# Bias of the output projection on VectorE, gate behind it on GpSimd, and another rule for the order of TensorE's work

## What is computed

```python
xn = layernorm(x)                                   # x: 4 x 2048 x 256, no affine part
q, k, v = split(xn @ w_qkv + b_qkv)                 # 16 heads of 16
scores = where(j >= i, q @ k.T / 4, -inf)           # each token sees itself and what comes later
s = softmax(scores) @ v  ->  @ w_out + b_out
h = concat([xn, -xn]); h = relu(s0 * (h @ +-k0)) * 2
h = relu(s1 * (h @ +-k1)) * 2
g = silu(s2 * (h @ +-k2))                           # k0, k1, k2: booleans read as +1 and -1
out = x + s * g
```

## Time and profile before

| | |
|---|---|
| median of 3 runs | 2306.75 us (2304.43 to 2308.47) |
| the profiled execution | 2308.26 us, its span 2306.4 us |
| busy: PE, DVE, ACT, POOL | 97%, 78%, 69%, 40% of the span |
| granted TensorE clock | 0.989 of full speed on average |

### The profile page before, as it was taken

The page is one execution under the profiler, slowest core; times in us unless marked ns, Lnnn a source line. Parts: engine busy times, 40 slices in busy tenths (PEclk is TensorE's granted clock), DMA queues, the critical chain, the costliest instruction groups (busy, mean ns, idle before and its releaser), DMA issues.

```text
span 2306.4 us, 60918 instructions
## 1 busy us (share of the span) xinstructions
PE 2228.7 (97%) x23760; PEld 1536.8 (67%) x23760; DVE 1808.4 (78%) x4514; ACT 1580.3 (69%) x3199; POOL 912.1 (40%) x1080
## 2 busy tenths in 40 slices
PE   7998999999999999999999999999999999999886
PEld 6887766666666666676676666666666666666553
DVE  7776788888888888888888888788878787888642
ACT  5663567777777777676777677777777675776573
POOL 1005334333343435343444435343443443354433
PEclk9999999999999999999999999999999999999997
DMA  8985102111111313131221312131312212222222
GB/s 306 357 316 174 43 23 57 32 46 41 52 45 38 95 46 93 37 85 54 79 60 44 88 47 82 44 94 42 86 46 52 86 45 72 59 84 70 75 77 80
DMA packets 157844, 193.31 MB, mean 84 GB/s; under 512 B 65276, under 2 KB 102076, under 8 KB 157560
## 3 DMA queue, kind: packets, MB, share of 16 engines
q1 hardware_dynamic: 156600, 189.41, 27.0%
q10 hardware_dynamic: 960, 0.00, 0.0%
HBM read 112.13 MB, written 76.14 MB: 82 GB/s over the span
## 4 chain that ended last, share of the span: by engine, by line
PE 83%; DMA 5%; DVE 4%; POOL 2%; issue 2%; ACT 2%; SPq 2%; ACTq 0%; POOLq 0%; DVEq 0%
PE b_ps L1437 25%; PE b_pv_ps L1403 22%; PE b_ps L1374 15%; PE b_ps L1384 11%; PE b_ps L1433 5%; DMA a_xs<-L_attn_x 3%; PE b_ps L1458 3%; DVE b_part_max L1549 1%; DVE a_stats L397 1%; ACT b_u L1523 1%; DVE a_qk_parts L435 1%; PE a_qk_ps L291 1%; PE b_ps L1391 1%; POOL b_u_lo L1303 1%; ACT b_probs L1492 1%
## 5 line engine op out<-in xcount | busy, mean ns | idle before, releaser
L1492 ACT ACTIVATE b_probs<-b_ps 128x512 f32<-128x512 f32 (+3 forms) x2560 | 1258.2, 537 | 585.0 <-PE b_ps L1374 554.0
L1549 DVE TENSOR_REDUCE b_part_max<-b_ps 128x1 f32<-128x512 f32 x1536 | 971.6, 680 | 175.0 <-PE b_ps L1384 168.4
L1384 PE MATMUL b_ps<-k_kst,k_qst 48*128 48x512 f32 (+3 forms) x2560 | 894.9, 390 | 10.4 <-DVE b_part_max L1546 4.0
L1374 PE MATMUL b_ps<-k_qst,k_kst 50*128 50x512 f32 (+3 forms) x2560 | 891.4, 389 | 1.1 <-ACT b_probs L1492 0.8
L1374 PEld LDWEIGHTS b_ps<-k_qst,k_kst 50*128 50x128 f32 x2560 | 431.7, 185 | 315.2 <-DVE b_part_max L1549 115.5
L1546 DVE CUSTOM_DVE_ANT_0 b_ps<-b_ps,k_mask 128x512 f32<-128x512 f32 (+3 forms) x1024 | 483.2, 512 | 155.6 <-PE b_ps L1384 149.4
L1403 PE MATMUL b_pv_ps<-b_probs,k_vst 128*32 128x512 f32 (+3 forms) x5120 | 598.9, 542 | 1.9 <-issue 1.7
L1437 PE MATMUL b_ps<-b_u_hi,k_w 64*128 64x256 f32 x4096 | 585.8, 280 | 2.4 <-ACT b_u L1523 0.9
L1437 PE MATMUL b_ps<-b_u_lo,k_w 64*128 64x256 f32 x4096 | 584.0, 279 | 0.0
L1384 PEld LDWEIGHTS b_ps<-k_kst,k_qst 48*128 48x128 f32 x2560 | 432.3, 185 | 139.3 <-DVE b_part_max L1549 44.3
L1437 PEld LDWEIGHTS b_ps<-b_u_hi,k_w 64*128 64x128 f32 x4096 | 456.0, 186 | 21.0 <-ACT b_z L1514 4.3
(11 more groups left out here) (103 smaller groups left out, 1920.8 us busy)
## 6 DMA issues: line engine op xcount, KB each, us to landing
qk_parts<-a_qk_parts SPq DMA_DIRECT2D x64, 512.0 KB, 3.7
k_kst<-qk_parts SPq DMA_DIRECT2D x384, 64.0 KB, 2.3
k_qst<-qk_parts SPq DMA_DIRECT2D x384, 64.0 KB, 2.3
a_xs<-L_attn_x SPq DMA_DIRECT2D x16, 512.0 KB, 5.9
xn_T<-a_xT SPq DMA_DIRECT2D x16, 512.0 KB, 5.8
v_plain<-a_v_out SPq DMA_DIRECT2D x16, 512.0 KB, 5.6
k_xf<-xn_T SPq DMA_DIRECT2D x32, 256.0 KB, 3.3
b_v_in<-v_plain SPq DMA_DIRECT2D x64, 128.0 KB, 2.6
```

The lines of the kernel that those rows point to most:

```text
L1374: pe.matmul(dst[:, 0:cols], keys, qst[rows, c, pair, 0:cols], start=True, stop=True).then_inc(s_ready, 1)
L1384: pe.matmul(dst[:, 0:CHUNK - k1], qst[rows, c, pair, i * P:(i + 1) * P], kst[rows, k_slot(kc, g % 2), pair, k1:CHUNK], start=True, stop=Tr ...
L1492: act.activation(probs[:, s % P_SLOTS, h, 0:cols], ps[:, banks[place, 0][0], 0:cols], ACT.Exp, scale=HD ** -0.5).then_inc(exp_done, 1)
L1549: dve.tensor_reduce(dst, src, AX_X, ALU.max).then_inc(ring_read, 1)
```

## The change

Two things, in one diff.

**The combine.** VectorE now adds the bias as it reads the projection out of PSUM, into `heads_T`, whose columns have been used by then (`projected(half)`); that is its only operation there. GpSimd multiplies it by the gate and adds `xs` (`finish`), behind the projection. Nothing is put in `inv` any more but the inverses, so the spread waits for nothing but their store. The heads' fetch stands first; it waits for the `finish` of the chunk before (`y_ready`). The fetch of gate and x stands behind it and waits, as before, for the store of the chunk before. The steps at which the events stand are moved by 0 to 3. The last chunk, of which three quarters are projected ahead, has events of its own (`fetch_last`, `finish_last`).

**The order.** `ROUND` is gone. `choose` takes values as soon as four steps wait, and, once it is at values, goes on while over two wait (`LEFT` = 2); else network if that is behind its schedule; else rows if banks are free; else network; else values, but not where a row pair is 0.3 us away by its own clock.

```diff
-COMBINE = (("fetch", 0), ("fetch_heads", 0), ("bias", 2), ("invert", 3), ("spread", 5), ("scale", 7), ("project", 10))
-COMBINE_LATE = (("fetch", 0), ("fetch_heads", 0), ("bias", 2), ("invert", 2), ("spread", 4), ("scale", 6),
-                ("project", 8))
+COMBINE = (("fetch_heads", 0), ("fetch", 1), ("invert", 3), ("spread", 5), ("scale", 8), ("project", 11), ("finish", 13))
+COMBINE_LATE = (("fetch_heads", 0), ("fetch", 0.5), ("invert", 2), ("spread", 3), ("scale", 5), ("project", 7),
+                ("finish", 8))
...
-               (base + 21, last + 2, COMBINE_LATE), (base + 30, last + 1, COMBINE_LATE), (base + 37, last, GATE_PARTIAL)]
+               (base + 21, last + 2, COMBINE_LATE), (base + 31, last + 1, COMBINE_LATE), (base + 36, last, GATE_PARTIAL)]
...
-    WAITING, LEFT = 4, 3
+    WAITING, LEFT = 4, 2
...
     def choose(self):
-
         now = self.clock["PE"]
         rows, at = self.rows_from(now)
         behind = self.network_behind()
-        network = self.network_from() <= now
+        network = self.network_from() <= now and behind > -self.SLACK
         products = self.products_from() <= now
         waiting = self.scores // GH - self.products
-        last = self.scores == GH * TOTAL
-        for _ in self.ROUND:
-            turn = self.ROUND[self.turn % len(self.ROUND)]
-            if turn == "R" and rows:
...
-        if network and behind > -self.SLACK:
+        if products and (waiting >= self.WAITING or self.mode == "V" and waiting > self.LEFT):
+            return "V"
+        if network and behind > 0:
             return "F"
-        return "V" if products else None
+        if rows and at <= now:
+            return rows
+        if network:
+            return "F"
+        if products and not (rows and at <= now + 0.3):
+            return "V"
+        return None
...
-                    if e != PARTIAL_HEADS:
-                        sp.wait_ge(bias_done, 2 * (t + 1))
...
+                elif what == "finish":
+                    e, i, half = arg
+                    if half == 1:
+                        sp.wait_ge(y_ready, 2 * (e + 1))
                         sp.dma_start(tokens(out_t, i), xs[:]).then_inc(y_stored, DMA)
...
-                        pool.tensor_tensor(at, gate[:, rows], bo[:].unsqueeze(1).to_broadcast([P, FPU, H]), ALU.mult
-                                           ).then_inc(gated, 1)
...
+                    pool.wait_ge(based, 2 * e + half + 1)
+                    pool.tensor_tensor(projected(half), projected(half), gate[:, rows], ALU.mult).then_inc(gated, 1)
                     pool.wait_ge(gated, 2 * e + half + 1)
-                    pool.tensor_tensor(tokens, tokens, at, ALU.add).then_inc(bias_done, 1)
+                    pool.tensor_tensor(xs[:, rows], xs[:, rows], projected(half), ALU.add).then_inc(y_ready, 1)
...
-                    dve.wait_ge(bias_done, 2 * (t + 1))
-
-                    dve.wait_ge(scaled, KH * (e + 1))
-                    dve.tensor_tensor(gated_bias[:, rows], src, gate[:, rows], ALU.mult).then_inc(ring_read, 1)
+                    dve.tensor_tensor(dst, src, bo[:].unsqueeze(1).to_broadcast([P, FPU, H]), ALU.add).then_inc(ring_read, 1)
                     dve.wait_ge(ring_read, uses)
-                    dve.tensor_tensor(xs[:, rows], xs[:, rows], gated_bias[:, rows], ALU.add).then_inc(y_ready, 1)
+                    dve.sem_inc(done, 1)
```

More of the change, by code:

```diff
@@ L601, in side_events @@
             e = heads if what in ("fetch_heads", "invert", "spread", "scale") else tokens
-            if what in ("bias", "scale"):
+            if what == "finish_last":
+                out += [(t + gap + half, 1.0 + 0.001 * n, what, half) for half in range(2)]
+            elif what == "fetch_last":
+                out.append((t + gap, 3.7, what))
+            elif what in ("finish", "scale"):
                 out += [(t + gap + half, 1.0 + 0.001 * n, what, e, i, half) for half in range(2)]
@@ L605, in side_events @@
                 out += [(t + gap + half, 1.0 + 0.001 * n, what, tokens, heads, i, half) for half in range(2)]
-            elif what == "spread":
-                out.append((t + gap, 3.7 + 0.001 * n, what, tokens, heads, i))
             else:
                 out.append((t + gap, 3.7 + 0.001 * n, what, e, i))
-        tokens += stages is not PARTIAL
+        tokens += stages not in (PARTIAL, GATE_PARTIAL)
         heads += stages is not GATE_PARTIAL
@@ L729, in beside @@
             else:
-                if what == "fetch" and self.due:
+                if what in ("fetch", "fetch_heads") and self.due:
                     self.whole_array()
-                if what in ("bias", "scale", "place_v", "gate"):
-                    self.clock["POOL"] += {"bias": 2.5, "scale": 1.3, "place_v": 0.5, "gate": 1.3}[what]
+                if what in ("finish", "finish_last", "scale", "place_v", "gate"):
+                    self.clock["POOL"] += {"finish": 2.5, "finish_last": 2.5, "scale": 1.3, "place_v": 0.5, "gate": 1.3}[what]
                 elif what in ("recip", "invert"):
@@ L1098, in chunk_of, with projected @@
             return CPB - 1 - c
+        def projected(half):
+            return heads_T[:, :, half * PIECE:(half + 1) * PIECE]
         def f_bank(use, n):
@@ L1185, in _ @@
                     else:
-                        sp.wait_ge(y_ready, 2 * e)
                         sp.wait_ge(o_stored[i % CPB], (GROUPS - 1) * O_STORES * DMA)
@@ L1218, in _ @@
                     rows = slice(half * FPU, (half + 1) * FPU)
-                    sp.wait_ge(y_ready, 2 * (NCHUNK - 1) + half + 1)
+                    sp.wait_ge(last_y, half + 1)
                     sp.dma_start(tokens(out_t, LAST_CHUNK)[:, rows], last_xs[:, rows]).then_inc(y_stored, DMA)
                 elif what == "project":
-                    t, e, i, half = arg
                     uses += 1
-                    if half == 1 and e != PARTIAL_HEADS:
-                        sp.wait_ge(y_ready, 2 * (t + 1))
+                elif what == "finish":
+                    e, i, half = arg
+                    if half == 1:
+                        sp.wait_ge(y_ready, 2 * (e + 1))
                         sp.dma_start(tokens(out_t, i), xs[:]).then_inc(y_stored, DMA)
@@ L1316, in _ @@
                         pool.tensor_copy(bv_wide[:, k, :], bv[:, k:k + 1].to_broadcast([P, P])).then_inc(bv_spread, 1)
-                elif what == "bias":
+                elif what == "finish":
                     e, i, half = arg
```

90 lines of the change are left out of this document (35 added, 55 removed).

## The result

The kernel after takes **2289.39 us** (median of 4 runs, 2288.98 to 2290.60), the kernel before 2307.56 (4 runs, 2304.43 to 2308.47). The ratio is 0.9926, 95% interval 0.9912 to 0.9939: 18 us or 0.8% less, where I had forecast 38 us or 1.6%. The profiled execution has a span of 2288.8 us.

A forecast was written before the change was run, and what follows sets the result against it. The prediction took TensorE's own issue sequence as the bound: 2308.3 - 49.5 (visits) + 36 (bank waits) - 24 (combine) = 2270.8, less 1.5 to the median: 2269 us. Forecast band 2252 to 2286, range 2242 to 2302.

The forecast's parts named there:

- rivals 2 and 3: Whole kernel: the combine gains nothing, or a pair's second values step pays its entry; 2287 to 2301 us, chance 0.17 together.
- part 3: The combine, from 1500 us on: projections wait less for scaled heads and the end's rounds about fit their steps; -24 us.
- the round at the end: Last group's combine, counted from heads to heads: 24 us instead of 35.0, about fitting the 10 steps the order leaves.
- part 2: TensorE's new waits for banks behind values pairs: 239 more places with nothing to issue at 0.15 us; +36 us.
- rival 3: Values pairs: the second step pays its entry, so visits save 28.5 instead of 49.5 us; 2290 us, chance 0.17 with rival 2.
- part 1: TensorE's order: 150 fewer visits to values (runs of consecutive values steps) at 0.33 us each; -49.5 us.
- rival 2: Combine at the end: round still longer than its 10 steps, projections wait as before; 2293 us, chance 0.17 with rival 3.
- third rival: The same as rival 3: the second values step of a pair pays its entry; 2290 us.
- fifth rival: Whole kernel: nothing moves, waits grow to match the visits, each near 0.3 us, +72 us; 2305 us, chance 0.07.
- first rival: VectorE becomes the bound in bursts: each of 166 values pairs costs TensorE 0.60 us, +100; 2333 us, chance 0.10.
- The condition that I named and did not price: SP's queue: the forecast is wrong if waiting for `y_ready` makes keys, queries or row maxima late; no size given.
- What would show it: Signs in the after trace, such as 1.86 us for 1024 values columns and projections' wait for GpSimd under 2 us a time.

The follow-up runs named there:

- combine_only: The kernel after with the fixed round of before (RRFRRV, LEFT = 3), so only the new combine; 2291.19 us, ratio 0.9939 to before.
- left3: The kernel after with LEFT = 3 instead of 2, so never a second values step behind the first; 2338.05 us, ratio 1.0137 to before.
- neg_act: The kernel after with the four DMAs of the last row maxima issued from ScalarE's queue, not SP's; 2284.39 us, ratio 0.9902 to before.
- round_all: combine_only with the last row-maxima DMAs on ScalarE's queue and SP's store and wait for finished tokens two steps later; 2287.39 us, ratio 0.9921 to before.

## Why the prediction was right or wrong

The time fell, but by just under half of the forecast: 18 us measured, 38 forecast. 2289 us lies outside the forecast's band (2252 to 2286) and inside the one that I had given to rivals 2 and 3 with 0.17. Two steps failed. In part 3 it is the round at the end, which I put at 24 us and said to fit about into its steps: it took 32.7, and of the 15 us forecast for the last group combine_only shows none. In part 2 it is the term of +36 us, which came out at some +50. That rival 3's 2290 us is met to 1 us is luck, since its mechanism is out (part 1). Of rival 2 the half that the last round doesn't fit held, the half that the projections wait as before didn't (5.7 us, before 14.8). By the parts:

**Part 1, fewer visits: right.** -49.5 forecast. left3 has 161 visits more than after and 24 places fewer, and takes 49 us longer, where 0.33 us a visit makes 53. The pair of 1024 columns takes the predicted 1.86 us, so the third rival (the entry is paid twice) is out. By the rule of the Trainium skill that I had set beside it ("TensorE: Matmul & The Clock Gate", section "The mechanism") it would be 2.0 us (an estimate, 1.86 and another entry of 0.14); the measurement decides.

**Part 2, waits for banks: the price and the count too small.** I put 239 places at 0.15 us, +36; the 25 more at the head (51 to 76) are in the 239, and the 31 more in the last group I left to part 3, where no term stands for them. Against combine_only the six kernels with the new rule are left with 0.16 to 0.20 us a place; 289 x 0.17 = +49. Of the 13 us that are missing, 239 x 0.02 = 5 are the price and 50 x 0.17 = 8 the count: 31 places of the last group, and 19 because combine_only has 97 places where before has 116. Against combine_only the order also saves 157 visits, not 150: -51.8 + 50.0 = -1.8, which is the measured difference again, since the price comes from it. Measured by itself, the order is worth 2 us on top of the combine and 6 alone. That is the fifth rival's mechanism, waits that grow until they match the visits, which I had given 0.07. The first rival stayed out: per values pair the waits are 50 / 166 = 0.30 us, under its point of 0.44. That all of the 50 are waits for banks is not shown; some 20 are seen in the trace.

**Part 3, the combine: too large.** -24 forecast, -16 measured by combine_only. In the body it gave more than I said: by step 600 combine_only is 16 us ahead, where I had 8.6 (11.6 idle less 3). From 1500 us on combine_only is visibly idle for 4.7 us (620 - 615.29, below) where before has 11.6 in its 640 us. So some 7 of the 16 are idle time that is gone.

```profile
1500.00:2120.00 620.00, 615.29 (x6866) 413.94 (x6862) 504.79 (x1247) 448.75 (x918) 269.37 (x315) 1.00 0.24 69
```

Nearly all of the rest is the clock, which I had not priced. The kernel before stalls twice in this stretch. Once VectorE waits for the sums that it is to invert, and TensorE for VectorE; once the projection waits for the heads:

```profile
1797.25 0.55 DVE L1582 RECIPROCAL b_sums<-b_sums 128x64 f32<-128x64 f32 x1 [3.67 <-DMA b_sums<-sums]
```

```profile
1798.51 0.79 PE L1384 MATMUL b_ps<-k_kst,k_qst 48*128 48x512 f32 x1 [3.17 <-DVE b_part_max L1546]
...
1949.09 3.75 PE L1458 MATMUL b_ps<-b_wo,b_heads_T 128*128 128x256 f32 x8 [3.77 <-POOL b_heads_T L1341]
```

Around and behind each stall the granted clock is down to the level of 1.2 GHz:

```profile
1797.50:1804.50 7.00, 5.99 (x36) 3.90 (x38) 4.45 (x14) 2.13 (x4) 4.53 (x4) 0.51 0.45 117
1947.50:1954.50 7.00, 5.41 (x16) 2.73 (x16) 1.56 (x2) 0.00 (x0) 6.26 (x8) 0.52 0.00 0
```

That is 14 us at about half the rate, 7 us of work. combine_only has neither stall, and its clock is 1.00 in the whole stretch. 7 us of idle time and 7 of clock make 14 of the 16.

In the last group the combine gave nothing where I had 15: the body's 16 us are all that combine_only's median has, and its profiled execution even fell back by 7 there (-16.4 at step 600, -9.2 at the last sums), behind its 8.1 us wait. There the failed step is the round of 24 us. Measured in after, from one sums' issue to the next (2214.70 to 2247.36), it is 32.7, and in neg_act, where TensorE doesn't wait for row maxima, 29.4 (2213.25 to 2242.64); before it was 35.0:

| piece | forecast | after | neg_act |
|---|---|---|---|
| sums' issue to inverses' store | 4.8 | 6.2 (2214.70 to 2220.94) | 4.1 |
| its landing, to the spread's issue | 2.0 | 3.4 (to 2224.29) | 6.5 |
| spread to its landing | 6.8 | 5.9 (to 2230.15) | 5.8 |
| two scalings | 2.6 | 2.5 (to 2232.66) | 2.5 |
| until the projection's turn | 0 | 6.0 (to 2238.68) | 0.2 |
| two projections | 3.7 | 3.7 (to 2242.40) | 5.3 |
| VectorE, GpSimd, store | 4.0 | 4.5 (to 2246.86) | 4.5 |
| store to the next sums' issue | 0 | 0.5 (to 2247.36) | 0.5 |

Rows of the scalings and of the projections, GpSimd and TensorE of the kernel after:

```profile
2230.15 2.51 POOL L1327 TENSOR_TENSOR b_heads_T<-b_heads_T,b_inv 128x512 f32<-128x512 f32 x2 [9.85 <-DMA b_inv<-inv_sums]
...
2241.61 1.27 POOL L1311 TENSOR_TENSOR b_heads_T<-b_heads_T,b_gate 128x512 f32<-128x512 f32 x1 [8.95 <-DVEq L1581]
```

```profile
2238.68 3.72 PE L1444 MATMUL b_ps<-b_wo,b_heads_T 128*128 128x256 f32 x16
```

In after the chain of work was nearly as forecast; 6.0 of the missing 8.8 us are scaled heads that wait for their place in the order, `project` 7 steps behind the fetch, while TensorE had lost 7.2 us for row maxima. The steps were not 2.1 to 2.4 us long but 3.3. I had added up ScalarE's work and put no stall on it. In neg_act TensorE is there first, and the chain of work is itself 5 us longer than the forecast: the inverses' store takes 6.5 us to land and let the spread go, where I had 2.0 from a store of another size, and the projections run at a lowered clock. Why that landing takes 6.5 us there and 3.4 in after, no run shows.

**The condition that I named and did not price** came true: "if SP waits for `y_ready` so long that keys, queries or row maxima come late". It cost 5 us by neg_act's time, once in the program.

**What would show it.** Right: 1.86 us for 1024 columns; longer idle pieces of VectorE (1.06 us in the one shown); no wait of TensorE names the gate or the sum; the body shorter, from step 40 to 600 by 22 us (I had said 10 to 20), of which combine_only has 18. Wrong: the projections' wait is 2.9 us a time (5.7 / 2), not under 2, though only 2 are left of 4. Not counted: the 150 fewer row pairs of 0.34 us. No run singles out the 1 us for VectorE's and GpSimd's sharing either.

**The sum, put right:** 2308.3 - 49.5 + 49 - 16 = 2291.8, less 1.5: 2290 us, against 2289.4 measured. The 16 is measured, and the 49 is what the measured times leave over at 0.33 us a visit, so the sum had to come out; it is no forecast and no proof of the price.

## What to carry over

- When a rule of order trades switches against waits, price both at the same point and over the whole program, head and tail too: here, against the combine alone, 157 saved visits of 0.33 us paid for 289 new places of some 0.17, and 2 us were left.
- Price a chain of dependent stages and the steps that its events are given together: the later of the two decides. In after the scaled heads lay ready for 6.0 us because TensorE had stalled; with that stall gone (neg_act) TensorE waited 3.5 us for the heads, and only 5 us of the time were won.
- Price a stall of TensorE with what the clock takes behind it: two stalls of 3.2 and 3.8 us in the kernel before cost some 7 us more in this way.
- A wait that moves to the front of SP's DMA queue costs what happens to be queued behind it. Look for the one urgent transfer there and issue it from another queue; of 107 us of SP's waiting the runs show a cost of 5 us, through one group of four DMAs.

## What the runs showed of the hardware

**The clock after a stall.** Behind the 7.2 us wait for row maxima the granted clock is 0.50, which is the level of 1.2 GHz of the two (1.2 and 2.4), for some 9 us in which TensorE is busy, and then returns. Stretches of the kernel after:

```profile
2216.00:2224.00 8.00, 0.85 (x8) 0.19 (x8) 0.55 (x1) 1.46 (x5) 4.13 (x5) 0.75 0.80 236
2224.00:2233.00 9.00, 8.71 (x48) 5.93 (x50) 0.00 (x0) 7.15 (x15) 2.51 (x2) 0.50 0.22 63
2233.00:2245.00 12.00, 12.00 (x104) 7.69 (x102) 1.39 (x2) 5.86 (x13) 3.32 (x3) 0.97 0.05 12
```

Network pairs start 0.21 us apart in the middle stretch (2228.49 to 2228.70) and 0.12 afterwards (2233.79 to 2233.91):

```profile
2228.49 0.42 PE L1419 MATMUL b_ps<-k_w,b_u_lo 64*128 64x256 f32 x2
2228.70 0.42 PE L1419 MATMUL b_ps<-k_w,b_u_hi 64*128 64x256 f32 x2
...
2233.79 0.28 PE L1419 MATMUL b_ps<-k_w,b_u_hi 64*128 64x256 f32 x2
2233.91 0.28 PE L1419 MATMUL b_ps<-k_w,b_u_lo 64*128 64x256 f32 x2
```

Nine us at half the rate are 4.5 us of work lost, besides the 7.2 of the stall. Yet neg_act, which has neither, gained only 5 of these 11.7 us: it was 9.9 us ahead at step 628 and lost 5 of them at once, 3.5 to the projections' wait for the heads and 1.6 to the clock behind that wait.

**Executions of one kernel** differ by 0.1% for after (2288.98 to 2290.60, at mean clocks of 0.988 and 0.989) and by 0.5 to 0.7% for combine_only (2288.07 to 2299.99) and round_all (2280.21 to 2295.09). In these two the time follows the mean granted clock:

| | time (mean clock) of each execution |
|---|---|
| combine_only | 2299.99 (0.989), 2295.29 (0.989), 2291.19 (0.992), 2288.96 (0.994), 2288.07 (0.994) |
| round_all | 2295.09 (0.988), 2289.11 (0.991), 2285.67 (0.993), 2280.21 (0.995) |

By an estimate from these numbers, 0.005 of 2290 us is 11 us of TensorE's work, where combine_only spreads over 12, and 0.007 is 16, where round_all spreads over 15. In the trace of combine_only, its longest execution, the clock is 0.85 from 2120 to 2198 us, where the 8.1 us wait for queries stands, and 0.96 in after. Whether the shorter executions lack that wait is not known, as none of them has a trace, and neg_act's longest (2285.90) has its highest clock (0.992), so the clock isn't all. It bears on the comparison above: the two executions of combine_only at after's clock took 2295 and 2300 us, 6 to 11 more than after, so what the order is worth on top of the combine is less sure than the medians' 2 us.
